# Cross attention with feature-major q and k, fp32 scores in four row groups, and its first batch prepared inside the MLP

## The reference, cut to what matters

```
x = x + attn(layernorm(x))                       # rms, q k v, cumulative sums, then a SwiGLU MLP with 2048 hidden
# the part that the change is about:
h = layernorm(x)                                 # without scale and shift
q = (h @ w_q.T).reshape(B, S, 8, 4, 16)          # 8 groups x 4 heads x 16
k = (ctx @ w_k.T).reshape(B, S, 8, 16)           # one k and one v for each group
v = (ctx @ w_v.T).reshape(B, S, 8, 16)
scores = einsum('bnghd,bmgd->bnghm', q, k) / 4   # 32 heads, 256 x 256, causal, padding mask
out = einsum('bnghm,bmgd->bnghd', softmax(scores), v)
x = x + out.reshape(B, S, 512) @ w_o.T + b_o
x = x + moe(layernorm(x))                        # a shared expert for all, and the top 2 of 8 experts
```

## Time and profile before

| | us |
|---|---|
| median of 3 runs | 1556.99 (1556.44 to 1557.81) |
| the profiled execution, its own time | 1556.8 |
| its span, first to last instruction | 1555.1 |
| MLP's last matmul ends, about | 740.2 |
| first scores of the cross attention | 772.87 |
| starts of passes 1 to 7 | 817.84, 868.15, 918.34, 968.61, 1018.79, 1068.96, 1119.14 |
| last scores | 1162.50 |
| first transposes of the MoE's loop (`m_t(0)`) | 1196.49 |
| busy over the span: PE, DVE, ACT, POOL | 1441.3, 732.1, 629.2, 367.1 |

### The profile page before, as it was taken

The page is one execution under the profiler, slowest core; times in us unless marked ns, Lnnn a source line. Parts: engine busy times, 40 slices in busy tenths (PEclk is TensorE's granted clock), DMA queues, the critical chain, the costliest instruction groups (busy, mean ns, idle before and its releaser), DMA issues. The chain is left out here.

```text
span 1555.1 us, 21990 instructions
## 1 busy us (share of the span) xinstructions
PE 1441.3 (93%) x7360; PEld 1095.8 (70%) x7360; DVE 732.1 (47%) x2017; ACT 629.2 (40%) x1359; POOL 367.1 (24%) x392
## 2 busy tenths in 40 slices
PE   5999979999999999999689999999987979999995
PEld 4888868888888888888567777777755866444442
DVE  4788753334234233333677766776655572000000
ACT  3444421111111111111298888888881222333331
POOL 4555440202102020120111110110022112444442
PEclk9999989999999999999899999999997998999998
DMA  6000020101011010100100000000004612454543
GB/s 243 1 0 0 0 90 33 41 1 41 0 41 41 0 40 0 41 17 0 31 18 19 18 1 19 18 5 2 25 18 183 271 61 75 83 93 83 94 83 46
DMA packets 20363, 73.02 MB, mean 47 GB/s; under 512 B 2288, under 2 KB 3312, under 8 KB 17840
## 3 DMA queue, kind: packets, MB, share of 16 engines
q0 software_dynamic: 10176, 25.17, 8.2%
q1 hardware_dynamic: 10096, 46.66, 8.1%
HBM read 52.69 MB, written 19.14 MB: 46 GB/s over the span
## 5 line engine op out<-in xcount | busy, mean ns | idle before, releaser
L683 PE MATMUL ps<-feat,wsplit 128*128 128x512 f32 x512 | 201.5, 394 | 9.0 <-POOL wsplit L573 3.7
L1270 ACT ACTIVATE sc<-sc,mxs 128x256 f32<-128x256 f32 (+1 forms) x512 | 199.3, 454 | 3.9 <-DVE mxs L1636 2.9
L684 PE MATMUL ps<-feat,wsplit 128*128 128x512 f32 x512 | 200.4, 391 | 0.0
L685 PE MATMUL ps<-feat,wsplit 128*128 128x512 f32 x512 | 200.3, 391 | 0.0
L1143 ACT ACTIVATE sg<-ps 128x512 f32<-128x512 f32 x64 | 38.3, 598 | 380.4 <-PE ps L685 380.4
L1636 DVE CUSTOM_DVE_ANT_0 sc<-ps,msk 128x256 f32<-128x256 f32 (+1 forms) x512 | 154.4, 353 | 58.6 <-PE ps L931 54.1
L1382 DVE TENSOR_TENSOR m_f<-ps,sg 128x512 f32<-128x512 f32 x64 | 44.2, 691 | 256.7 <-ACT sg L1143 256.7
L1051 PE MATMUL ps<-rawx,hT_x 128*128 x312 | 143.7, 603 | 1.0 <-issue 0.6
L1837 DVE TENSOR_TENSOR m_x<-ps,sgx 128x256 f32<-128x256 f32 x55 | 23.3, 424 | 230.5 <-ACT sgx L1338 230.2
L1276 ACT COPY pt<-ps 128x512 f32<-128x512 f32 x192 | 112.4, 585 | 45.0 <-PE ps L939 44.5
L939 PE MATMUL ps<-ident,sc 128*128 128x128 f32 x768 | 117.3, 275 | 13.0 <-ACT sc L1270 11.8
(11 more groups left out here) (265 smaller groups left out, 2851.7 us busy)
## 6 DMA issues: line engine op xcount, KB each, us to landing
wraw<-weights SPq DMA_DIRECT2D x11, 1536.0 KB, 6.4
rawx<-weights SPq DMA_DIRECT2D x8, 1536.0 KB, 12.7
ctx_raw<-ctx_t SPq DMA_DIRECT2D x8, 512.0 KB, 4.5
h_rows<-hd POOLq DMA_DIRECT2D x16, 256.0 KB, 2.6
out<-acc SPq DMA_DIRECT2D x4, 1024.0 KB, 4.3
acc<-x SPq DMA_DIRECT2D x1, 3584.0 KB, 19.5
qkv_raw<-weights SPq DMA_DIRECT2D x6, 512.0 KB, 7.8
msk_i<-mask SPq DMA_DIRECT2D x8, 128.0 KB, 3.6
```

The costliest lines, as they stand in the source:

```text
L683: nc.tensor.matmul(out_, w_hi, m_hi, start=first, stop=False)
L684: nc.tensor.matmul(out_, w_lo, m_hi, start=False, stop=False)
L685: return nc.tensor.matmul(out_, w_hi, m_lo, start=False, stop=last)
L1270: ins = nc.scalar.activation(cols, cols, ACT.Exp, bias=mxs[:, u % 4, n:n + 1], scale=-1.0)
```

## The change

- q and k are made feature-major: weights are the stationary operand, `hTc` and `ctx_s` the moving one. The pieces `kT` (12 matmuls of 256 columns), `v` (24 of 128 columns), `qT0` and `qT1` (24 of 256 columns each) take the place of `kv`, `q0` and `q1`. All transposes of q4 and k4 go. DVE copies q once, and k twice, each time with one group of every pair of groups set to zero (`half_of`).
- Scores are plain fp32 with a contraction of 32 rows (two groups of 16, one of which is zero in k). Four units are a set: `scores(b, s)` fills banks 0 to 3 from row groups 0 to 3, 4 matmuls of 512 columns or 8 of 256. It waits until all maxima of the set before it are taken. `sc` and `pt` get 8 places.
- For the 8 units with four blocks POOL subtracts the maximum (`less_max`), and ACT takes one Exp of 512 columns instead of four of 128.
- hT and oT are copied out of PSUM by ACT and split by POOL; POOL adds the bias to x; the two bias matmuls of a tile go.
- Transposes go through banks 4 and 5 (`TURNED` and the units, four units after their scores), sums over v through bank 6, and projections and the `n` pieces through bank 7 (`SUMMED`, one semaphore `sum_read`).
- The first batch's transposes of h, its k and v are made ahead of the MLP's last `down`, its q right behind it.
- There is no pass without units: the last units of batch 7, the first six `head_t`, `up_d(0)` and `up_d(1)` are written in one order, and the last output projection lies behind `down_d(0)`.
- x comes in three DMAs; DVE's `batch_a(0)` waits for tiles 2 and 3 alone (`x_second`). The zero rows are stored behind the weight splits.

```
-PIECES = {0: "n10", 1: "k4Tb", 2: "kv", 3: "hT0", 4: "q4T13", 5: "hT1", 7: "n11", 8: "q0",
-          9: "n00", 10: "oT0", 11: "oT1", 12: "q4T00", ..., 15: "q4T03", 16: "q1",
-          17: "wo0", 18: "n01", 19: "k4Ta", 20: "q4T10", 21: "wo1", 22: "q4T11", 23: "q4T12"}
+TURNED = {1: "hT0", 2: "hT1", 10: "oT1", 18: "oT0"}
+SUMMED = {0: "n2", 3: "kT", 6: "v", 8: "n3", 11: "qT0", 12: "n0", 14: "wo1", 16: "n1", 19: "qT1", 22: "wo0"}
...
-            sp.dma_start(acc[:, TPB:TILES, :], x_v[:, TPB:TILES, :]).then_inc(x_rest, 16)
+            sp.dma_start(acc[:, TPB:2 * TPB, :], x_v[:, TPB:2 * TPB, :]).then_inc(x_second, 16)
+            sp.dma_start(acc[:, 2 * TPB:TILES, :], x_v[:, 2 * TPB:TILES, :]).then_inc(x_rest, 16)
...
+            def less_max(b, u):                                   # POOL
+                pool.wait_ge(c["mx"], UNITS * b + u + 1)
+                nc.gpsimd.tensor_tensor(out=s_u, in0=m_u, in1=s_u, op=ALU.subtract).then_inc(c["sub"], 1)
+            for b in range(BATCH):                                # POOL, one batch
+                less_max of units 0 to 3; hT_split(b + 1, 0); less_max of units 4 to 7; hT_split(b + 1, 1)
+                if b == 0:
+                    pool.wait_ge(c["wo_hi"], 1)
+                    nc.gpsimd.tensor_tensor(out=wsplit[:, 1, 1, :], in0=wraw[:, 1, :], in1=wsplit[:, 1, 0, :], op=ALU.subtract).then_inc(w_ready[1], 1)
+                else:
+                    oT_split(b - 1, 1)
+                add_bias(b); ctx_split(b + 2); rstd_c(b + 2); (b == 7: split(0, SLOT_MOE // 2, base)); oT_split(b, 0)
...
+            def keys(bank):                                       # PE
+                for kb in range(KB):
+                    mm = three(pe, bank[:, 0:SEQ], slot_block(0, 0, o, P), slot_block(0, 1, o, P), ctx_s[:, 0, kb, :], ctx_s[:, 1, kb, :], kb == 0, kb == KB - 1)
+            def values(bank):
+                for t in range(TPB):
+                    for kb in range(KB):
+                        mm = three(pe, bank[:, n], ctx_s[:, 0, kb, n], ctx_s[:, 1, kb, n], slot_block(0, 0, o, P), slot_block(0, 1, o, P), kb == 0, kb == KB - 1)
+            def queries(half, bank):
+                for i in range(2):
+                    for kb in range(KB):
+                        mm = three(pe, bank[:, i * SEQ:(i + 1) * SEQ], slot_block(0, 0, o, P), slot_block(0, 1, o, P), hTc[:, 0, kb, :], hTc[:, 1, kb, :], kb == 0, kb == KB - 1)
+            def first_pieces(qs):
+                if qs:
+                    pe.wait_ge(c["hT"], TPB)
+                    for half in range(2):
+                        queries(half, ps[:, 2 + half, :])
+                    return
+                pe.wait_ge(mlp["m"], JB * CHUNKS * MLP_GROUPS)
+                for t in range(TPB):
+                    turn_h(0, t, ps[:, 2 + t, :])
+                pe.wait_ge(w_ready[0], SLOT_X // 2 + 1)
+                pe.wait_ge(c["ctx_s"], 1)
+                keys(ps[:, 0, :])
+                values(ps[:, 1, :])
+            def scores(b, s):
+                after(pe, c["mx"], UNITS * b + 4 * s)
+                for n in range(2 if s < FIRST_SETS else 1):
+                    for j in range(4):
+                        rows = slice(32 * j, 32 * j + 32)
+                        if s < FIRST_SETS:
+                            mm = nc.tensor.matmul(ps[:, j, n * SEQ:(n + 1) * SEQ], qT[rows, 4 * pb + 2 * s + n, 0:P], kd[rows, 2 * pb:2 * pb + 2, 0:P], start=True, stop=True)
+                        else:
+                            mm = nc.tensor.matmul(ps[:, j, :], qT[rows, 4 * pb + s - FIRST_SETS, P:SEQ], kd[rows, 2 * pb:2 * pb + 2, :], start=True, stop=True)
+            def attend(b, s):                                     # per 128 queries: 2 x 4 matmuls of 256 columns, or 4 x 4 of 128
+            def pass_c(b):
+                for u in range(UNITS):
+                    if u % 4 == 0:
+                        scores(b, u // 4)
+                    turned_piece(TURNED[u], b) and summed_piece(SUMMED[u], b), where u has one
+                    turned_piece(f"p{u}", b)                      # probs_t of the unit four back
+                    if u % 4 == 1:
+                        attend(the set two and a quarter back)
...
+            summed_piece("n2", BATCH)                             # PE, behind the last pass
+            turned_piece p0, p1; attend(BATCH - 1, 4); head_t(0); head_t(1); turned_piece p2, p3
+            head_t(2); head_t(3); attend(BATCH - 1, 5)
+            up_d(0)
+            summed_piece("n3"); head_t(4); head_t(5)
+            m_t(0); up_d(1); turn_o(BATCH - 1, 1, ps[:, 5, :]); down_d(0); summed_piece n0, wo1; head_t(6); then the loop from i = 1
...
+                if s_u has four blocks (units 0 to 7):            # ACT, exps
+                    nc.scalar.activation(s_u, s_u, ACT.Exp).then_inc(c["P"], 1)
...
+            def heads_read(b, n):                                 # DVE, the n pieces
+                if b == 0 and n == 0:
+                    dve.wait_ge(w_ready[1], SLOT_X // 2 + 1)
+            steps(..., meanwhile={1: first_norm, 2: first_rows, 3: first_pieces})   # DVE, in the MLP's last group
```

More of the change, by code:

```diff
@@ L350, in decoder_layer @@
         c = signals(
-            "c_", wo_hi="the output weights' hi", ctx_hi="the first context's hi", ones="v's columns of ones and zeros", zeros="the halves of k4T that stay zero",
+            "c_", wo_hi="the output weights' hi", ones="v's columns of ones and zeros", half="the two masks of rows",
             ctx="contexts loaded, by 16", ctx_s="contexts split", mask_i="masks loaded, by 16", pad="masks of padding",
-            mask="masks made", stats="batches whose mean and variance are made", rstd="batches whose scales are made",
@@ L354, in decoder_layer @@
-            h="tiles normalised", hT_ps="tiles of h transposed in PSUM", hT_hi="their hi", kv_ps="batches with k | v in PSUM",
-            kv_hi="their k's hi", k4T_ps="halves of the pairs of split k transposed in PSUM", q_ps="tiles of q in PSUM", q_hi="their hi",
-            q4="tiles of q split and doubled", q4T_ps="quarter tiles of q4 transposed in PSUM",
-            oT_ps="tiles of o transposed in PSUM", oT_hi="their hi", wo_ps="tiles of the output projection in PSUM",
-            S="units with scores in PSUM", mx="units with masked scores and their maximum", P="units of probabilities",
@@ L359, in decoder_layer @@
-            PT_ps="units transposed in PSUM", PT="units transposed in SBUF", O="fours of units summed over v",
-            o_raw="quads' tiles copied out", n_ps="quads' tiles transposed back", rden="their reciprocal row sums",
+            mask="masks made", bias="the bias loaded, by 16", biased="tiles with the bias in the residual",
+            stats="batches whose mean and variance are made", rstd="batches whose scales are made",
+            h="tiles normalised", hT_ps="tiles of h transposed in PSUM", hT_first="the first batch's copied out", hT="tiles of h transposed and split",
@@ new lines, in decoder_layer @@
+            kT_ps="batches with k^T in PSUM", v_ps="batches with v in PSUM", q_ps="halves of q^T in PSUM", first="the first batch's k, v and q in SBUF",
+            oT_ps="tiles of o transposed in PSUM", oT_hi="the last one's hi", oT="tiles of o transposed and split", wo_ps="tiles of the output projection in PSUM",
+            S="sets with scores in PSUM", mx="units with masked scores and their maximum", sub="units less their maximum", P="units of probabilities",
+            PT_ps="units transposed in PSUM", O="sets summed over v",
@@ L361, in decoder_layer @@
+            o_raw="heads' sums copied out", n_ps="heads' sums transposed back", rden="their reciprocal row sums",
             pool="GpSimd's own small steps", dve="the vector engine's")
[L362 removed]
+        sum_read = sem("c_sum_read")
+        turned = [sem(f"c_turned{k}") for k in range(2)]
         d = signals(
```

914 lines of the change are left out of this document (484 added, 430 removed).

## The result

The changed kernel takes 1478.24 us (median of 4 runs, 1477.27 to 1479.17) beside 1557.4 for the kernel before on the same chip: a ratio of 0.948, 95% interval 0.947 to 0.9495. Run again beside later kernels it took 1478.09 (5 runs, ratio 0.948, 0.9461 to 0.9499). The forecast was 1472, its own range 1456 to 1486, so the time lies inside, 6 us above the forecast. The sum hides a term that was 10 us off, and smaller ones the other way.

A forecast was written before the change was run, and what follows sets the result against it. PE's work was taken to bound a steady pass. Gains of 4 (start), 21 (MLP's end), 4.9 (pass 0), 28.8 (passes 1 to 6) and 30.8 (pass 7 with tail), minus 5, took 84.5 off 1556.8: 1472 us, own range 1456 to 1486.

The forecast's parts named there:

- What bounds the kernel: Steady cross-attention pass: PE's work sets its cost, busy 47.28 of 50.19 us, with ACT close behind at 43.10.
- Scores: Six sets a steady pass at 1.1 us each, row groups running at once; 3.5 a set if one after another.
- Attend: Sums over v in a steady pass: six at 6.2 us together, up to 1.0 more each if bound by instructions.
- Rival 4: Attend with 128 columns is bound by instructions: +4 x 8 = 30 less what lies in waits, 1498; chance 6%.
- Steady pass: Passes 1 to 6 of the cross attention: 45.4 us each instead of 50.2, 42.0 of it PE's work.
- my remainder of 3.4: Waits and gaps of PE in a steady pass: 3.4 us instead of 4.3, bounds 2 and 7.
- Pass 0: First attention pass: 45.4 less 7.8 for missing earlier-batch work, plus 2.5 for its own wait: 40.1 us.
- The start and the MLP's end: Kernel start gains 4 us as DVE's wait for x goes; MLP's end to first scores gains 21, 32.7 to 11.7.
- Rival 3: The ends don't close: first scores and MoE wait for chains, stores and splits, 18 of 46 us lost, 1490; chance 12%.
- Pass 7 with the tail: Last pass, 34.6 us without the next batch's pieces, and tail of 12 to `m_t(0)`: 46.6 instead of 77.4.
- Given back: Behind `m_t(0)`: turn_o and wo1 (3.2) and a chain through ACT and DVE (2) cost 5 us.
- Rival 1: In `scores`, row groups run one after another: 3.5 instead of 1.1 us a set, +115, 1587; chance 8%.

The follow-up runs named there:

- experiment 3: Changed kernel with every scores matmul issued twice in a row into the same place: 1515.84 us, one run.
- experiment 2: Changed kernel with the four matmuls of a set of scores sharing two row groups: 1517.52 us, one run.
- experiment 1: Changed kernel with all four matmuls of a set of scores reading partitions 0 to 31, one row group: 1735.07 us, one run.
- experiment 8: Changed kernel with ScalarE again taking the maximum off in its Exp, four of 128 columns for one of 512, instead of GpSimd: 1489.47 us.
- experiment 5: Changed kernel with VectorE's three statistics groups moved from the last pass, tile by tile, into the pass before: 1475.83 us.
- experiment 4: Changed kernel with 9.8 us of unread stand-in matmuls in the last pass where the next batch's pieces are missing: 1486.22 us.
- experiment 6: On top of experiment 5, VectorE makes seven of ScalarE's copies of transposed probabilities in the last pass: 1475.94 us.
- experiment 10: Changed kernel with the first batch's h transposes, k and v behind the MLP's last down instead of ahead of it: 1480.71 us.

## Why the prediction came out as it did

**What bounds the kernel** held: PE's work is what a steady pass costs. The added copies of experiment 3 and the halved packing of experiment 2 are paid to 0.1 us. How the 5.5 us won in a steady pass divide between the transposes that are gone, the scores and the waits is counted from rows, here as in the prediction; no run puts the transposes of q and k back.

**Scores.** The term of 1.1 us a set, taken from `attend` against a bound of 3.5, measured 1.07. Experiments 1 to 3 fit one line: 0.21 us for a visit and 0.43 for each instruction of 512 columns that has to wait its turn (8, 4 and 2 of them: 3.64, 1.91, 1.07). By the figure of the Trainium skill, TensorE: Matmul & The Clock Gate, Part 3, a set was estimated at 1.14; measured, four row groups beat one by 3.64 / 1.07 = 3.4 where the page has 3.07, and without the 0.21 by 4. The Trainium skill, TensorEngine Tiling (Array Packing), Key Properties, says that a change of mode drains the array; the 0.21 agrees in kind, and is more than the 0.12 that I read from `attend`.

**Attend** with 128 columns takes 1.01 us from start to next start (1064.04 to 1065.05 in the last pass), as with 256. Rival 4 is out (its 4 x 8 is 32, not 30; the forecast doesn't hang on it).

**Steady pass.** 44.7 for 45.4. PE is idle for only 0.5 us. The largest part of my remainder of 3.4 that I can place stands in the pieces: eight transposes take 0.97 (893.23 to 894.20) and not 0.86, four behind a visit 0.49 and not 0.43, near 1.8 us for 32 fours. ACT came out at 33.7 (33.5 forecast), DVE at 28.1 (28.7), POOL at 22.3 (28): `less_max` takes 1.04 us and a copy 0.61, where I took 1.32 for both. I judged ACT by its total; experiment 8 shows that its place in the first two sets was the nearest bound.

**Pass 0** 38.7 for 40.1; PE is idle for 38.68 - 36.37 = 2.3 us there, 1.8 more than in a steady pass, against the 2.5 that I had given; the other 0.7 is the cheaper steady pass.

**The start and the MLP's end.** Forecast 4 and 21, measured 2.8 and 20.7. At DVE's first row on the residual the gain is 4.1 (24.12 to 20.02); 1.3 of it is gone by the MLP. Rival 3 is out at this end.

**Pass 7 with the tail** is the mis-sized term: 46.6 forecast, 56.5 measured. I took pass 7 as a steady pass less the 10.8 us of the pieces that it lacks, 34.6. That holds only while PE is the bound, and those pieces were the cover that made it so. Measured 40.7: 3.4 for DVE's statistics, a moved step that I had not costed (experiment 5), and some 3 for rounds through the other engines (0.74 + 0.79 + 0.88 + 0.65 = 3.1) that nothing hides (experiments 4 and 6). The tail took 15.8 for 12.0. Its waits are 1.83, 0.98 and 0.34, 3.2 together, and I had allowed 2 for all latencies. Another 1.5 us are the clock: behind the wait of 1.83 us, 32 `attend` and 8 `head_t` instructions took 1.75 and 1.76 us to the next start at a granted clock of 0.55 and 0.50 (1.2 GHz), instead of 1.01 and 1.05 at the upper level. Behind the same wait in the second profile the clock stayed at 1.00. The last 1.1 us or so are pieces that each take a little more than I had counted. Rival 3 had its price here, 10 of its 18 us, though not by the stores and splits that I named.

That the total still lies 6 us from the forecast is in part luck: passes 0 to 6 came out 5.5 us better than forecast, for a smaller remainder of waits and gaps than I had allowed, and paid for half of this error.

**Given back** behind `m_t(0)`: 5 forecast, 5.7 measured.

**Rival 1** did not occur, but its price was wrong as well: 1587 by the sets alone, 1735 in experiment 1, because of the clock.

## What to carry to other kernels

A pass that lacks a part of its work need not be shorter by that part (here 10.8 us of work were missing, and the pass was 4.0 shorter): take off the work, then look for what it covered, with each engine's list in order. A busy share over a pass does not clear an engine: ACT at 83% of a pass was the bound in its first two sets of six, and moving 4.6 us a pass off it was worth 11 in the whole. Work for a later stage belongs into a pass that another engine bounds, and not into the last one.

## What the runs showed of the hardware

- Four fp32 matmuls of 32 rows in four row groups run at once: two instructions of 512 columns each, 0.43 us a turn, plus 0.21 a visit. Two groups cost twice the turns, one four times (1.07, 1.92 and 3.64 us for a set).
- With one row group in use for 3.64 us the granted clock fell from 1.00 to 0.55 in the stretch behind it, and was 0.74 over the pass; with two it stayed at 1.00. A pass so costs 18 us more than the serial matmuls themselves, with PE busy throughout.
- GpSimd takes 1.04 us to subtract 128x512 from a maximum that is broadcast over blocks, 1.27 us for a plain subtraction or sum of that size in the same pass.
- The MLP's start varies from 229.6 to 233.4 us between profiles of kernels that are alike up to there. In the stretch from 200 to 229 us the granted clock was 0.94 in the earliest (experiment 10) and 0.83 in the changed kernel's profile, whose MLP starts 2.8 us later:

```profile
200.00:229.00 29.00, 25.25 (x114) 20.86 (x115) 17.75 (x13) 6.67 (x10) 10.60 (x3) 0.94 0.31 115
```

```profile
200.00:229.00 29.00, 25.20 (x101) 20.49 (x102) 17.73 (x12) 6.04 (x9) 10.62 (x3) 0.83 0.28 109
```

That spread is as large as what several of the experiments measured, so those are read by the lengths of stretches first and not by the medians alone.
